# Attention with relative positions: the sum of values in four steps, reciprocals turned in the rows' PSUM region, repeated thirds copied by GpSimd

## The reference, cut to what matters

```python
q = (x @ Wq + bq).reshape(B, S, H, dh)
k = (x @ Wk + bk).reshape(B, S, H, dh)
v = (x @ Wv + bv).reshape(B, S, H, dh)
p = (pe @ Wpos).reshape(S, H, dh)
content_score = jnp.einsum('bshd,bthd->bhst', q + u_bias, k)
pos_score = jnp.einsum('bshd,thd->bhst', q + v_bias, p)
pos_score = rel_shift(pos_score)
score = (content_score + pos_score) / np.sqrt(D).astype(np.float32)
attn = jax.nn.softmax(score, axis=-1)
ctx = jnp.einsum('bhst,bthd->bshd', attn, v).reshape(B, S, D)
return ctx @ Wout + bout
...
top_w, top_i = jax.lax.top_k(gate_logits, TOP_K)
top_w = jax.nn.softmax(top_w, axis=-1)
```

## Time and profile before

| what | value |
| --- | --- |
| median of 3 runs | 3697.31 us (3690.72 to 3698.98) |
| profiled execution | 3699.55 us, span 3697.8 us |
| busy over the span | PE 3040.4 us (82%), DVE 2724.1 (74%), ACT 2193.0 (59%), POOL 704.1 (19%) |
| moved by DMA | 1022.91 MB, mean 277 GB/s |
| position rows' first and last step | about 1263 to 3048 us of the span |

### The profile page before, as it was taken

One profiled execution on the slowest core, in us unless ns is written; L12 is line 12 of the kernel. 1 busy time (PEld: TensorE's weight loads), 2 busy tenths in 40 slices (PEclk: granted clock), 3 DMA queues, 4 the chain that ended last, 5 costly groups with the idle time before them and its releaser, 6 DMA issues. The chain is left out here.

```text
span 3697.8 us, 75688 instructions
## 1 busy us (share of the span) xinstructions
PE 3040.4 (82%) x28916; PEld 2329.6 (63%) x28916; DVE 2724.1 (74%) x5210; ACT 2193.0 (59%) x3568; POOL 704.1 (19%) x760
## 2 busy tenths in 40 slices
PE   3788888888467588888888888889888883999994
PEld 2555555556356367776667767677666672777773
DVE  4888888887454278878888888788787884776674
ACT  2455565555355366676666766666666661776670
POOL 1000000000011001121220221211221203566561
PEclk9899999999777699999999999999999996999995
DMA  2446446446377799999999999999999993777776
GB/s 60 123 167 196 130 165 196 135 160 186 123 286 277 255 371 361 375 371 368 370 364 369 377 375 376 370 365 370 366 364 376 373 337 111 241 248 260 243 234 273
DMA packets 290942, 1022.91 MB, mean 277 GB/s; under 512 B 51620, under 2 KB 57520, under 8 KB 281574
## 3 DMA queue, kind: packets, MB, share of 16 engines
q1 hardware_dynamic: 273382, 985.32, 75.6%
q0 software_dynamic: 17280, 33.87, 2.4%
HBM read 486.24 MB, written 489.85 MB: 264 GB/s over the span
## 5 line engine op out<-in xcount | busy, mean ns | idle before, releaser
L954 ACT ACTIVATE att_skewed<-att_skewed,att_neg_max 128x1024 f32<-128x1024 f32 x512 | 588.9, 1150 | 425.7 <-DVE att_neg_max L1095 424.6
L1095 DVE CUSTOM_DVE_ANT_0 att_skewed<-att_score_ps,att_skewed 128x1024 f32<-128x1024 f32 x512 | 625.6, 1222 | 121.1 <-issue 105.2
L1211 PE MATMUL att_turn_ps<-att_ident,att_skewed 128*128 128x128 f32 x4096 | 576.6, 286 | 144.1 <-ACT att_skewed L954 142.5
L1211 PEld LDWEIGHTS att_turn_ps<-att_ident,att_skewed 128*128 128x128 f32 x4096 | 469.9, 145 | 326.7 <-ACT att_skewed L954 307.1
L945 ACT ACTIVATE att_rows<-att_wide_ps 128x1152 f32<-128x1152 f32 x512 | 573.3, 1120 | 125.5 <-PE att_wide_ps L1175 125.0
L1103 DVE COPY att_turned<-att_turn_ps 128x1024 f32<-128x1024 f32 x512 | 624.8, 1220 | 9.6 <-PE att_turn_ps L1211 9.1
L1175 PE MATMUL att_wide_ps<-att_ps,att_qs 98*128 98x128 f32 (+3 forms) x1920 | 434.3, 347 | 22.7 <-DVE att_token L987 15.6
L909 POOL DMA_INDIRECT expert_rows<-att_expert_rows,att_place x256 | 247.8, 968 | 808.6 <-DVE att_place L1053 721.1
L1203 PE MATMUL att_score_ps<-att_ks,att_qs 96*128 96x512 f32 x1024 | 368.4, 442 | 32.5 <-DVE att_neg_max L1095 29.4
L1175 PEld LDWEIGHTS att_wide_ps<-att_ps,att_qs 98*128 98x128 f32 x1920 | 310.1, 200 | 76.0 <-issue 31.7
L155 POOL DMA_INDIRECT expert_parts<-exp_parts,exp_rows x284 | 299.1, 1053 | 207.4 <-ACT exp_parts L186 141.4
(11 more groups left out here) (263 smaller groups left out, 5196.4 us busy)
## 6 DMA issues: line engine op xcount, KB each, us to landing
skewed_rows<-att_rows SPq DMA_DIRECT2D x512, 576.0 KB, 6.7
att_skewed<-skewed_rows SPq DMA_DIRECT2D x512, 512.0 KB, 7.6
expert_rows<-conv_pad SPq DMA_DIRECT2D x144, 520.0 KB, 11.0
exp_weights<-split_weights SPq DMA_DIRECT2D x71, 1028.0 KB, 6.8
att_qs<-queries SPq DMA_DIRECT2D x192, 128.0 KB
att_ks<-keys SPq DMA_DIRECT2D x192, 128.0 KB
exp_rows<-expert_rows SPq DMA_DIRECT2D x71, 260.0 KB, 2.9
sum_part<-expert_parts SPq DMA_DIRECT2D x32, 512.0 KB, 7.3
```

The lines of the kernel that those rows point to most:

```text
L954: act.activation(skewed[r % RING][:], skewed[r % RING][:], ACT.Exp, bias=neg_max[:, k:k + 1], scale=-1.0, accum_out=sums[:, k:k + 1]).then ...
L1095: dve.tensor_tensor_reduce(skewed[r % RING][:], score_ps[:], skewed[r % RING][:], -SCALE, 3.0e38, ALU.add, ALU.min, neg_max[:, k:k + 1]).t ...
L1211: last = pe.transpose(turn_ps[:, t * P:(t + 1) * P], skewed[r % RING][:, t * P:(t + 1) * P], ident[:])
```

## The change: order, places and loads

Four things change in `attention_phase`, and the lags and step numbers with them.

1. The sum of values of a tile is no longer one run of 32 products at lag 7. It is cut into four pieces of eight products, one in each of the steps at lag 7, 8, 9 and 10. The context product, the output product and the addition follow at lags 11, 11 and 12 (before 8, 8 and 9).
2. The transposition of the reciprocals leaves the bank of the sums. PE makes it at lag 8, ahead of the position rows, in the last 128 columns of the spare region (`recip_ps`), and ACT copies it ahead of its copy of the rows.
3. Of each stack only the two different thirds are loaded from HBM (except for the first image). GpSimd copies the third that repeats, for all heads at once, one copy for q and one for k (`repeat_high`), between normalising and the scatter of the rows.
4. q is issued in steps 8 to 14, k in steps 16 to 22, v in 26, x in 17; routing runs two or three steps later than before.

```diff
-LOAD_Q_AT, LOAD_K_AT, LOAD_V_AT = (12, 14, 16, 18), (20, 22, 24, 26), 28
-LOAD_X_AT = 14
-ROUTE_AT, STATS_AT, OFFSET_AT, NORMED_AT, POWER_AT, PLACES_AT, ROUTE_END = 9, 10, 15, 18, 24, 27, 30
-GATES_AT = (22, 23, 24, 25, 28)
-S_LAG, EXP_LAG, TURN_LAG, VALUES_LAG, OUT_LAG, ADD_LAG = 5, 5, 6, 7, 8, 9
+LOAD_Q_AT, LOAD_K_AT, LOAD_V_AT = (8, 10, 12, 14), (16, 18, 20, 22), 26
+LOAD_X_AT = 17
+ROUTE_AT, STATS_AT, OFFSET_AT, NORMED_AT, POWER_AT, PLACES_AT, ROUTE_END = 12, 13, 17, 20, 26, 29, 32
+GATES_AT = (24, 25, 26, 27, 30)
+S_LAG, EXP_LAG, TURN_LAG, VALUES_LAGS, RECIP_LAG, OUT_LAG, ADD_LAG = 5, 5, 6, (7, 8, 9, 10), 8, 11, 12
...
+        recip_ps = spare[:, 2 * P:3 * P]
...
             def load_q(n, b, h):
-                for j, half in enumerate((0, 1, 0)):
-                    sp.dma_start(raw(qs[b][j * DH:(j + 1) * DH, h, 0:T]), q_dram[n, half, h * DH:(h + 1) * DH, :]).then_inc(inputs_loaded[b], 16)
+                part = slice(h * DH, (h + 1) * DH)
+                sp.dma_start(raw(qs[b][0:DH, h, 0:T]), q_dram[n, 0, part, :]).then_inc(q_high_loaded[b], 16)
+                sp.dma_start(raw(qs[b][DH:2 * DH, h, 0:T]), q_dram[n, 1, part, :]).then_inc(inputs_loaded[b], 16)
+                if is_first(n):
+                    sp.dma_start(raw(qs[b][2 * DH:STACK, h, 0:T]), q_dram[n, 0, part, :]).then_inc(first_repeats, 16)
...
+            def repeat_high(n):
+                b = n % 2
+                pool.wait_ge(q_high_loaded[b], uses(n, b, HIGHS))
+                pool.tensor_copy(qs[b][2 * DH:STACK, :, 0:T], qs[b][0:DH, :, 0:T]).then_inc(q_repeated, 1)
+                pool.wait_ge(q_repeated, n)
+                pool.wait_ge(k_high_loaded[b], uses(n, b, HIGHS))
+                pool.tensor_copy(ks[b][DH:2 * DH, :, :], ks[b][0:DH, :, :]).then_inc(k_repeated, 1)
+                pool.wait_ge(k_repeated, n)
...
+            repeat_high(1)
             for m in range(NB):
                 route_rows(m)
+                if m + 2 < NB:
+                    repeat_high(m + 2)
+                scatter_rows(m)
...
                     if spared:
                         empty(spared[0], spared[2])
+                    if turned_tile:
+                        keep_recip(*turned_tile)
                     at_least(act, rows_written[s % ROWS], 16 * (STEPS // ROWS * n + s // ROWS))
                     act.activation(rows[s % ROWS][:], wide_ps[:, 0:WIDE], ACT.Copy).then_inc(wide_read, 1)
...
-            def sum_values(m, b, r):
+            def turn_recip(m, b, r):
+                pe.wait_ge(recip_ready, TT * m + r // HEADS + 1)
+                return pe.transpose(recip_ps, recip[:].rearrange("p h d -> p (h d)"), ident[:])
+
+            def sum_values(m, b, r, piece):
                 G = TT * m + r // HEADS
-                pe.wait_ge(recip_t_ready, G + 1)
-                pe.wait_ge(turn_read, STEPS * m + r + 1)
+                if piece == 0:
+                    pe.wait_ge(turn_read, STEPS * m + r + 1)
+                    at_least(pe, context_ready, G)
+                if piece == 1:
+                    at_least(pe, out_added, G)
                 first = r % (2 * HEADS) + 1 - HEADS
-                for t in range(TT):
+                each = TT // len(VALUES_LAGS)
+                for t in range(each * piece, each * (piece + 1)):
...
-                at = last_of_tile(n, b, s, TURN_LAG)
-                if at:
-                    G = TT * at[0] + at[2] // HEADS
-                    pe.wait_ge(recip_ready, G + 1)
-                    at_least(pe, out_added, G)
-                    pe.transpose(tail_ps[:, P:2 * P], recip[:].rearrange("p h d -> p (h d)"), ident[:]).then_inc(recip_turned, 1)
...
+                ended, begun = last_of_tile(n, b, s, OUT_LAG), last_of_tile(n, b, s, VALUES_LAGS[0])
+                if ended:
+                    pe.wait_ge(context_ready, TT * ended[0] + ended[2] // HEADS + 1)
+                    last = pe.matmul(tail_ps[:, 2 * P:3 * P], wout[:], context[:], start=True, stop=True)
+                if begun:
+                    last = sum_values(*begun, 0)
...
```

More of the change, by code:

```diff
@@ L723, in attention_phase @@
         inputs_loaded, stored = [sem(f"inputs{b}_loaded") for b in range(2)], sem("stored")
+        q_high_loaded, k_high_loaded = ([sem(f"{s}_high{b}_loaded") for b in range(2)] for s in "qk")
+        first_repeats, q_repeated, k_repeated = sem("first_repeats"), sem("q_repeated"), sem("k_repeated")
         wide_filled, wide_read = sem("wide_filled"), sem("wide_read")
@@ L1200, in content @@
                 i, h = divmod(r, HEADS)
+                if r == 0 and not is_first(m):
+                    pe.wait_ge(k_repeated, m)
                 at_least(pe, score_read, STEPS * m + r)
@@ L1222, in sum_values @@
                                          start=(t == 0), stop=(t == TT - 1), skip_group_check=True)
-                last.then_inc(values_done, 1)
+                return last
             def slot(n, b, s):
```

65 lines of the change are left out of this document (44 added, 21 removed).

## The result

The changed kernel takes 3663.77 us in the median of five runs (3654.3 to 3677.4); the kernel before took 3697.31 beside it. The ratio is 0.9914 (95% interval 0.9886 to 0.9942): faster by 33.5 us, where 70 were forecast. The profiled execution of the changed kernel is the slowest of its five (3677.4 us, span 3675.6), so its stretches account for 22 of the 33.5 us; the shape is what they are read for.

The account below looks back on a forecast made before the run. A clean tile was taken as bound by a 12.50 us chain across engines, tiles 5 and 6 by transfers. Fifteen images at -4.5 us and the first at -2.9 gave -70: 3628 us, range 3565 to 3700.

Parts of the forecast that it names:

- the one on GpSimd's copies: Two copies an image on GpSimd, estimated at 4.2 us each, none of it on the path: taken as 0.
- The upper bound: For GpSimd's copies: the gating's DVE work is stretched by the whole 4.0 us of tile 7.
- For tiles 3 to 6 the working: Two loads fewer leave 20.5 MB, at 388 GB/s 52.9 us against 56.06: -3.2 us an image, bounds -0.6 and -4.8.
- Tile 1 was put at -0.1: Tile 1 of an image with routing, its DMA carrying the scattered rows as before: -0.1 us an image.
- the chain's term: Sum in four pieces shortens a chain-bound tile from 12.50 to 11.7 us; bounds 11.24 and 13.1; -0.5 counted in tile 2.
- The first image: It has no routing but loads the second image: 1.05 MB fewer at 357 GB/s, -2.9 us.
- The drain: The stretch behind the last image keeps its chain: 0, plus or minus 2 us.
- the term's lower bound of 15.8: Tile 7, with all gating but the last piece: DVE busy 15.8 us; forecast 17.2 (-0.5), bounds 15.8 and 18.5.
- the rival by which more comes free: Clock stays 1.00 in tiles 6 and 7, transfers at 400 GB/s: -7.5 us an image, 3584 us; chance 0.13.
- the slower rival: A piece behind every step's transposes delays the next position rows: +3.0 us an image, +48, 3748 us; chance 0.12.
- The rival with the DMA's mean rate: Transfers go at some 370 GB/s whatever the order, only bytes count: 2.8 us an image, 3654 us; chance 0.17.
- The rival that ends at 3690: GpSimd's copies stretch tile 7's gating by 4.0 us, eating 60 of the 70 us gained; chance 0.08.

Follow-up runs that it names:

- e14: Changed kernel with each GpSimd copy, from the third image on, reduced to 2 of a head's 1024 columns: 3622.13 us, ratio 0.9817.
- e4: Changed kernel with the sum of values in one run at lag 8 again, loads, copies and routing as changed: 3683.72 us, ratio 0.9978.
- e2: Changed kernel without GpSimd's copies, the repeated thirds loaded from HBM again in the changed steps: 3671.54 us, ratio 0.994.
- e1: Changed kernel with GpSimd's copy of k held back until DVE has done the fourth piece of the gating: 3629.14 us, ratio 0.9833.
- e3: Changed kernel with each of GpSimd's two copies cut into four, one per head: 3642.05 us, ratio 0.9864.
- e8: e1 with k loaded in steps 24 to 27 (tile 7), q in 12 to 18, v in 28, x in 22: 3583.9 us, ratio 0.9693.

## Why the prediction was wrong

**The step that failed** is the one on GpSimd's copies: "Nothing of it is on the path. ... I take 0". The copies cost 36 to 42 us (e14). The lower bound was taken because DVE's sum of durations in tiles 1 and 2 was alike with and without GpSimd. But GpSimd's 8.64 us in tile 1 are the scatter's issues (L909, nine of them), no copy, and these tiles hold the score and the copy from PSUM, which are not touched. The gating's operations were nowhere beside GpSimd in the trace, so the row said nothing of them. The trace of before did have the case, on another instruction: DVE's spreading copy L1087, 0.23 us, began beside GpSimd's running copy L904 in three images and took 0.86, 1.07 and 0.98, each time ending 0.08 behind it. Here is the fourth image:

```profile
L1087 DVE COPY att_recip<-att_recip_one x128: 226/227/1075, 1288.6 to 3064.2; 128x128 f32<-128x128 f32 x128
```

```profile
1646.12 1.04 POOL L904 COPY att_expert_rows<-att_expert_rows 128x1024 f32<-128x1024 f32 x1
1646.16 1.07 DVE L1087 COPY att_recip<-att_recip_one 128x128 f32<-128x128 f32 x1
```

The upper bound (4.0 us an image, 60 in all) was nearer: 42 / 14 = 3.0. The working even had k land "by tile 7", which is where it put the gates: the copy runs in steps 24 and 25, with the first of them.

The Trainium skill (GPSIMD Engine Reference, 8. Key points) names as contenders DVE instructions with two SBUF inputs or in a two-port mode. The trace agrees in kind with the first (L1054, two SBUF inputs, 0.21 to 3.55 us); L1123, a copy with one SBUF input, is held too (0.23 to 3.30), and whether it runs in such a mode no run here shows. The rule had been weighed and named the upper bound as its value; that was the better choice.

**The second error is the larger one and hid behind others.** For tiles 3 to 6 the working was 20.5 MB at 388 GB/s, 52.9 us; they took 57.15 on the mean, 56.17 without the copies. In the table that is +1.7 where -3.2 was forecast: 4.9 us an image, 68 us in 14 images. By the trace they moved 21.7 MB at 380. The working took the bytes of before and struck two loads. It left out that the shorter tiles 1 and 2 pass on what they don't move, that the scatter, two steps later, now fills these two (0.77 to 0.97 MB on the mean), and that the transfers which leave tiles 7 and 8 save nothing. So 1.2 MB (3.1 us) were missing, and 1.2 us came from the rate.

**What went better than forecast.** Tile 1 was put at -0.1 and gave 1.9: PE's own 11.28 us is its length, the lower bound of the chain's term. The first image gave 8.3 for 2.9, as the chain's gain counts there too (4.6 us by e4) and was counted in tile 2 alone; the thirds that it doesn't load gave more than the 2.9 (5.3 by e2; each counted alone). The drain held (23.1 to 23.2 us to attention's last addition). Without the copies tile 7 takes 15.6, near the term's lower bound of 15.8, not 17.2, at a mean granted clock of 0.99 where before it had 0.82: in that tile the rival by which more comes free was right. The misses add up: 68 us in tiles 3 to 6 and 38 by the copies, less 26 in tile 1, 24 in tile 7 without the copies and some 9 elsewhere, make up, but for rounding, the 48 us between the 70 forecast and the profile's 22. That the gains offset the second error is luck: e14's 3622 lies at the forecast's 3628 (its own sum gives 3627) for partly wrong reasons.

**The rest held.** The pieces shorten what stands between transposes and position rows (0.51 for 1.81 us), PE's wait for the reciprocals is gone, and its wait for exp fell by more than half, so the slower rival (a piece behind every step) was wrong. The rival with the DMA's mean rate had the number nearest to the result (3654) and not the mechanism: it counts each byte saved, and against the kernel before the megabyte saved counted for nothing, as it left tiles 7 and 8. In the same load steps it is worth 3.3 us an image in tiles 3 to 6 (e2 against e14). The rival that ends at 3690 had the mechanism, at two thirds of its price.

## What to carry to other kernels

Before work is given to an idle engine, look in the trace for instructions of other engines that stand while it runs (L1087 did), and work out at which step the new work will start: a copy that is off the path by its own waits can still hold the engine that is on it, for its whole length, and the remedy is to place it (e1) or to cut it (e3). A byte saved is worth its time only in a stretch that transfers bind; read the rate tile by tile, and move transfers into the stretch in which another engine binds (e8) before counting on fewer of them. When one stage gets faster, take the bytes it no longer has time to move and add them to the next one.
